# A three-layer interaction network on one core: one more group split by VectorE, a high-part ring of four, loop bodies of four steps

## What is computed

```python
for i, S in enumerate([128, 128, 128]):
    Wr = Ws[i].reshape(39, h.shape[1], S)
    out = relu(einsum('bfd,bgd,fgs->bsd', x, h, Wr) + bs[i][None, :, None])
    if i != 2:
        h, direct = out[:, :64], out[:, 64:]
    else:
        direct = out
    outs.append(direct)
return sum(concatenate(outs, axis=1), axis=-1)
```

## Time and profile before

| | |
|---|---|
| median of 3 runs | 571.18 us (571.01 to 573.93) |
| the profiled execution | 570.96 us, its span 569.1 us |
| busy, share of the span | PE 98%, DVE 93%, POOL 89%, PE's weight loads 66%, ACT 64% |
| granted PE clock | 0.996 of full speed |
| transfers | 121.68 MB, mean 214 GB/s |
| chain that ended last | PE 88%, POOL 5%, issue 3%, DMA, DVE and ACT 1% each |

### The profile page before, as it was taken

How to read it: one execution, slowest core, us unless ns; L and a number is a source line. 1 busy time by engine, 2 the same in 40 slices (tenths; PEclk the granted TensorE clock), 3 DMA queues, 4 the chain that set the end, 5 groups by cost and what they waited for, 6 DMA issues and landing times.

```text
span 569.1 us, 7814 instructions
## 1 busy us (share of the span) xinstructions
PE 558.0 (98%) x2003; PEld 377.6 (66%) x2003; DVE 531.8 (93%) x516; ACT 365.8 (64%) x409; POOL 505.5 (89%) x222
## 2 busy tenths in 40 slices
PE   8899999999999999999999999999999999999997
PEld 4354666767676666667767667676767766666765
DVE  5679999999999999999999999999999999999975
ACT  1255775766767576676776758586676757668562
POOL 1257999899999999999899999989999999999995
PEclk9899999999999999999999999999999999999999
DMA  8998935738375582846649285573837558262001
GB/s 331 412 413 329 383 115 181 299 124 332 101 261 225 179 332 85 311 157 203 276 146 346 68 295 214 166 313 113 329 111 256 229 173 337 79 210 80 0 2 37
DMA packets 27390, 121.68 MB, mean 214 GB/s; under 512 B 3312, under 2 KB 3440, under 8 KB 25328
## 3 DMA queue, kind: packets, MB, share of 16 engines
q1 hardware_dynamic: 27376, 121.52, 58.8%
HBM read 120.98 MB, written 0.52 MB: 213 GB/s over the span
## 4 chain that ended last, share of the span: by engine, by line
PE 88%; POOL 5%; issue 3%; DMA 1%; DVE 1%; ACT 1%; SPq 0%; POOLq 0%; DVEq 0%; ACTq 0%
PE acc L572 88%; POOL z_lo L294 4%; DMA xfirst<-x 1%; POOL w_lo L540 1%; DVE z_whole L431 0%; DVE z_raw L431 0%; ACT h L660 0%; ACT last L660 0%; ACT z_hi L657 0%; SPq L304 0%; SPq L327 0%; DVE z_hi L292 0%; ACT direct L660 0%; DVE sums L454 0%; DVE z_lo L291 0%
## 5 line engine op out<-in xcount | busy, mean ns | idle before, releaser
L294 POOL TENSOR_TENSOR z_lo<-z_raw,z_hi 128x1024 fp32r<-128x1024 f32 x202 | 477.8, 2406 | 25.2 <-ACT z_hi L657 22.7
L657 ACT CAST z_hi<-z_raw 128x1024 fp32r<-128x1024 f32 (+1 forms) x215 | 216.9, 1022 | 111.5 <-DVE z_raw L431 94.0
L431 DVE TENSOR_TENSOR z_raw<-h,xwide 128x1024 f32<-128x1024 f32 x189 | 225.6, 1214 | 4.7 <-ACT h L660 3.0
L572 PE MATMUL acc<-z_hi,w_hi 128*128 128x512 f32 (+1 forms) x543 | 210.1, 460 | 0.8 <-ACT last L660 0.8
L572 PE MATMUL acc<-z_hi,w_lo 128*128 128x512 f32 x530 | 171.7, 395 | 0.0
L572 PE MATMUL acc<-z_lo,w_hi 128*128 128x512 f32 x498 | 160.0, 397 | 2.3 <-POOL z_lo L294 1.9
L572 PEld LDWEIGHTS acc<-z_hi,w_hi 128*128 128x128 f32 (+1 forms) x543 | 102.2, 188 | 60.6 <-issue 39.5
L572 PE MATMUL acc<-z_whole,w_whole 128*128 128x512 f32 x256 | 120.0, 592 | 0.0
L572 PEld LDWEIGHTS acc<-z_hi,w_lo 128*128 128x128 f32 x530 | 99.4, 188 | 24.0
L572 PEld LDWEIGHTS acc<-z_lo,w_hi 128*128 128x128 f32 x498 | 92.6, 187 | 28.4 <-POOL z_lo L294 5.8
L431 DVE TENSOR_TENSOR z_whole<-h,xwide 128x1024 f32<-128x1024 f32 x68 | 82.3, 1213 | 6.2 <-PE acc L572 3.9
(11 more groups left out here) (25 smaller groups left out, 155.1 us busy)
## 6 DMA issues: line engine op xcount, KB each, us to landing
xwide<-x SPq DMA_DIRECT2D x160, 512.0 KB, 4.7
xfirst<-x SPq DMA_DIRECT2D x13, 2048.0 KB, 7.8
xfirst<-x SPq DMA_DIRECT2D x4, 768.0 KB, 12.2
xwide<-w SPq DMA_DIRECT2D x2, 1024.0 KB, 16.7
xwide<-x SPq DMA_DIRECT2D x1, 1280.0 KB, 11.8
xfirst<-x SPq DMA_DIRECT2D x2, 512.0 KB, 11.4
xwide<-x SPq DMA_DIRECT2D x1, 768.0 KB, 9.2
z_raw<-w0b SPq DMA_DIRECT2D x1, 640.0 KB, 6.0
```

The source lines that it names most:

```text
L294: return eng.tensor_tensor(lo[0:rows, 0:n, :], z[0:rows, 0:n, :], hi[0:rows, 0:n, :].bitcast(F32), ALU.subtract)
L431: nc.vector.tensor_tensor(dst, in0, in1, ALU.mult).then_inc(made[kind], 1)
L572: return nc.tensor.matmul(dst, w[0:rows, place, :], z[0:rows, t - G * g, :], start=first and first_g and t == G * g, stop=final and t == T ...
L657: nc.scalar.copy(z_hi[0:rows, slot("PV", pair, par, pos, HI_RING), 0:n, :], src).then_inc(hi_made, 1)
```

## The change

Layer 1's group 3 (position 3) becomes V instead of W. `z_hi` has four slots instead of six. The loop's body holds four steps and turns three times (a step has 19 P and V groups now, and a ring must fit into the loop body a whole number of times). In the first steps:

- Step 0 takes group 4 of layer 1 whole, with the raw weights, ahead of group 5; one P group less.
- Block 1's layer 0 is accumulated in `acc[2]`, so PE does not wait there for ACT to have read `acc[0]`; `relu0` reads it from there, and layer 2's first group in step 1 waits for that read.
- At the end of step 0 ACT runs `copy_xrep(1)` ahead of `relu0`.
- The split of layer 2's weights moves from position 2 of step 1 to position 0 on ACT and POOL, and on ACT ahead of `relu1`; their load moves ahead of one load of layer 0's operands in SP's queue.
- Layer 1 has 18 split weight tiles instead of 16 (and `w_whole` two less), so the staging areas in `xwide` shift and three `xwide` loads of block 1 wait for layer 2's split instead of two.

```diff
-KINDS = ("WPWP", "PWPWPPVPPV", "PPWPVPPWPV")
+KINDS = ("WPWP", "PWPVPPVPPV", "PPWPVPPWPV")
-ORDER_0 = "00W 01W 02W 03W 11W 13W 10W 12W 16W 14P 17W 15P 18P 19V"
-ORDER_1 = ("00W 01W 22W 27W 02W 03W 20P 10P 11W 21P 12P 23P 13W 14P 24V 15P 16V 25P 17P 18P 19V "
+ORDER_0 = "00W 01W 02W 03W 11W 13W 10W 12W 16W 14W 15P 17W 18P 19V"
+ORDER_1 = ("00W 01W 22W 27W 02W 03W 20P 10P 11W 21P 12P 23P 13V 14P 24V 15P 16V 25P 17P 18P 19V "
-SPLIT2_AT_1 = 2
-WHOLE_RING, RAW_RING, HI_RING, LO_RING = 4, 4, 6, 4
+SPLIT2_AT_1 = 0
+WHOLE_RING, RAW_RING, HI_RING, LO_RING = 4, 4, 4, 4
...
             load_first(2, xfirst_head_in[0], range(0, 1 + G))
+            sp.dma_start(stage[2][:, 0:SPLIT_COUNT[2], :], w2).then_inc(w_staged[2], 16)
             load_first(2, xfirst_head_in[1], range(1 + G, 1 + 2 * G))
-            sp.dma_start(stage[2][:, 0:SPLIT_COUNT[2], :], w2).then_inc(w_staged[2], 16)
...
-            with act.Fori(1, PAIRS - 1) as pair:
-                for par in range(2):
-                    step(pair, par)
+            with act.Fori(0, (BLOCKS - 4) // LOOP) as turn:
+                for par in range(LOOP):
+                    step(LOOP // 2 * turn + 1, par)
...
-                dst = acc[layer][:, :]
+                dst = acc[2 if isinstance(j, int) and (layer, j) == (0, 0) else layer][:, :]
...
-                    ready(pe, acc_read[layer], j + (1, 0, -1)[layer])
+                    if isinstance(j, int) and (layer, j) == (2, 1):
+                        pe.wait_ge(acc_read[0], 2)
+                    if isinstance(j, int) and layer == 0 and j < 2:
+                        ready(pe, acc_read[0], j)
+                    else:
+                        ready(pe, acc_read[layer], j + (1, 0, -1)[layer])
...
+                    if isinstance(j, int) and j == 1 and pos == SPLIT2_AT_1:
+                        split_layer(2)
                     if pos == RELU1_AT and has(1, BLOCKS):
-                        relu1(j, par)
+                        relu1(j, par % 2)
...
                 if isinstance(j, int) and j == 0:
-                    relu0(j, par)
                     copy_xrep(1)
+                    relu0(j, par % 2)
```

More of the change, by code:

```diff
@@ L20 @@
 PAIRS = BLOCKS // 2
+LOOP = 4
+assert LOOP % 2 == 0 and (BLOCKS - 4) % LOOP == 0
 BB = N // DIM
@@ L176 @@
 assert sorted(e[:2] for e in BEGIN[0]) == sorted(e[:2] for e in STEP if e[0] < 2)
-assert len(SPLIT0) > 0 and SPLIT_COUNT[1] <= 16 and SPLIT_COUNT[2] <= 16
+assert len(SPLIT0) > 0 and SPLIT_COUNT[1] <= 20 and SPLIT_COUNT[2] <= 16
 def cin(nc, x, x0, w0a, w0b, w1, w2, w_rest, b, out):
@@ L213, in cin @@
         z_psum = psum("z_psum", [128, G, N])
-        stage = [None, xwide[:, 1, T12 - 4:T12, :].rearrange("p a (b s) -> p (a b) s", s=SIZE),
-                 xwide[:, 1, T12 - 8:T12 - 4, :].rearrange("p a (b s) -> p (a b) s", s=SIZE)]
+        stage = [None, xwide[:, 1, T12 - 5:T12, :].rearrange("p a (b s) -> p (a b) s", s=SIZE),
+                 xwide[:, 1, T12 - 9:T12 - 5, :].rearrange("p a (b s) -> p (a b) s", s=SIZE)]
         xsecond = xwide[:, 1, 0:1 + T0, :]
@@ L263, in cin @@
         for kinds, ring in (("W", WHOLE_RING), ("P", RAW_RING), ("PV", HI_RING), ("PV", LO_RING)):
-            assert 2 * sum(e[2] in kinds for e in STEP) % ring == 0
+            assert LOOP * sum(e[2] in kinds for e in STEP) % ring == 0
         def place_of(j, layer):
@@ L339, in _ @@
             load_first(2, xfirst_head_in[0], range(0, 1 + G))
+            sp.dma_start(stage[2][:, 0:SPLIT_COUNT[2], :], w2).then_inc(w_staged[2], 16)
             load_first(2, xfirst_head_in[1], range(1 + G, 1 + 2 * G))
-            sp.dma_start(stage[2][:, 0:SPLIT_COUNT[2], :], w2).then_inc(w_staged[2], 16)
             load_first(2, xfirst_in, range(1 + 2 * G, 1 + T0))
             sp.wait_ge(*made_all(0, 0))
-            for g in range(G12 - 4):
+            for g in range(G12 - 5):
                 load_wide(1, 1, g)
@@ L352, in _ @@
             sp.wait_ge(w2_lo_made, 1)
-            for g in range(G12 - 4, G12 - 2):
+            for g in range(G12 - 5, G12 - 2):
                 load_wide(1, 1, g)
@@ L409, in products @@
                         dve.wait_ge(h_ready[0], 2 * (j + 1))
-                    dve.wait_ge(xw_in[1 - par][g], 16 * (pair + par + 1))
+                    dve.wait_ge(xw_in[1 - par % 2][g], 16 * (pair + par // 2 + par % 2 + 1))
                     in0 = h[0][:, None, :].to_broadcast([128, n, N])
-                    in1 = xwide[:, 1 - par, G * g:G * g + n, :]
+                    in1 = xwide[:, 1 - par % 2, G * g:G * g + n, :]
                 else:
@@ L416, in products @@
                     in0 = h[1][:, None, :].to_broadcast([128, n, N])
-                    in1 = xwide[:, par, G * g:G * g + n, :]
+                    in1 = xwide[:, par % 2, G * g:G * g + n, :]
                 number = before(kind, j, pos)
@@ L462, in step @@
                 if (not isinstance(j, int) or j > 1) and order(j - 1)[-1][2] == "V":
-                    late.append((V_LAG - 1, pair + par - 1, 1 - par, len(order(j - 1)) - 1))
+                    late.append((V_LAG - 1, *((pair, par - 1) if par else (pair - LOOP // 2, LOOP - 1)), len(order(j - 1)) - 1))
                 for pos, (layer, g, kind) in enumerate(order(j)):
@@ L467, in step @@
                     if pos == SUM1_AT and not (isinstance(j, int) and j < 1):
-                        sum_direct(j - 1, par)
+                        sum_direct(j - 1, par % 2)
                     if pos == SUM2_AT and not (isinstance(j, int) and j < 2):
@@ L502, in _ @@
                 step(0, par)
-            with dve.Fori(1, PAIRS - 1) as pair:
-                for par in range(2):
-                    step(pair, par)
+            with dve.Fori(0, (BLOCKS - 4) // LOOP) as turn:
+                for par in range(LOOP):
+                    step(LOOP // 2 * turn + 1, par)
             for par in range(2):
@@ L549, in _ @@
                 step(0, par)
-            with pool.Fori(1, PAIRS - 1) as pair:
-                for par in range(2):
-                    step(pair, par)
+            with pool.Fori(0, (BLOCKS - 4) // LOOP) as turn:
+                for par in range(LOOP):
+                    step(LOOP // 2 * turn + 1, par)
             for par in range(2):
@@ L635, in _ @@
                 step(0, par)
-            with pe.Fori(1, PAIRS - 1) as pair:
-                for par in range(2):
-                    step(pair, par)
+            with pe.Fori(0, (BLOCKS - 4) // LOOP) as turn:
+                for par in range(LOOP):
+                    step(LOOP // 2 * turn + 1, par)
             for par in range(2):
@@ L684, in relu0 @@
                     act.wait_ge(*made_all(j, 1))
-                a = acc[0]
+                a = acc[2 if isinstance(j, int) and j == 0 else 0]
                 relu(h[0][0:HALF, :], a[0:HALF, :], 0, slice(0, HALF)).then_inc(h_ready[0], 1)
@@ L715, in step @@
                     if pos == RELU0_AT and has(1, BLOCKS - 2):
-                        relu0(j, par)
+                        relu0(j, par % 2)
+                    if isinstance(j, int) and j == 1 and pos == SPLIT2_AT_1:
+                        split_layer(2)
                     if pos == RELU1_AT and has(1, BLOCKS):
-                        relu1(j, par)
+                        relu1(j, par % 2)
                     if pos == RELU2_AT and has(2, BLOCKS):
                         relu2(j)
-                    if isinstance(j, int) and j == 1 and pos == SPLIT2_AT_1:
-                        split_layer(2)
                     if kind != "W":
```

## The result

The changed kernel takes 580.69 us (median of 4 runs, 580.43 to 581.26) against 571.10 us; the ratio is 1.016, 95% interval 1.014 to 1.019. The forecast was 581.0 us and slower.

The account below looks back on a forecast made before the run. The loop through POOL, PE and ACT, at 34.80 us a step, was taken to bound the changed kernel: 570.96 + 12.6 for 13 steps - 2.6 for the first steps = 581.0 us, range 573.0 to 585.0.

Parts of the forecast that it names:

- PE 33.53: PE's work per step: position 3 as V instead of W saves 0.31 us, from 33.84 to 33.53.
- DVE 34.20: DVE's work per step: 33.07 us before plus one whole subtraction of 1.13 for position 3.
- the loop 34.80: Closed chain per step from POOL's position 0 through PE, ACT and back to POOL: 33.73 us plus 1.07.
- the added rounding: With four `z_hi` slots, ACT's rounding 20 waits for PE's position 16, ahead of `relu0`: 1.07 us more per step.
- 13 steps: POOL's position 0 in steps 2 to 15, 13 intervals of 34.80: 452.4 against 439.8 us, +12.6.
- first steps: Start: PE's removed wait and slow clock, earlier weight split, against later loads; bounds -1.4 to +4.6, gain of 2.6 us taken.
- from step 15's position 0 to the end of the span: The end: twelve POOL subtractions without a pause set PE's pace and layer 2 is unchanged; 0 us.
- That DVE sets the step: Rival: rounding 20 does not lengthen the loop, leaving DVE's 34.20 us a step; 573.2 us, chance 12%.
- That PE's saving counts: Rival: DVE fits the added 1.13 us into idle time, so PE's 33.53 a step holds; 563.9 us, chance 4%.
- That DVE stalls at the new subtraction: Rival: at position 3 DVE waits for rounding 3 behind `relu2`, making its step 35.27 us; 587.1 us, chance 8%.

Follow-up runs that it names:

- the six-slot kernel: The changed kernel with `z_hi` back at six slots and a loop body of all twelve steps; 572.67 us.
- the kernel with short sums and both moves: Changed kernel, six slots, 15 of 16 terms of each sum left out, `relu0`'s `direct` instruction and `relu2` moved later on ACT; 564.69 us.
- the changed kernel with `direct` moved: Changed kernel, four slots, `relu0`'s third instruction (writes `direct`) moved behind the rounding of the next step's position 0; 573.42 us.
- run 69: Not a label but a count: the kernel before, unchanged, was run 69 times beside the other kernels; from 569.2 to 574.2 us.

## Why the prediction was right

**The cause.** The step was forecast as the longest of three claims, PE 33.53, DVE 34.20 and the loop 34.80, and the loop won. Its links, forecast and measured: POOL's position 0 to PE's end of position 6, 12.44 and 12.47; PE's release of ACT, taken as PE's end plus 0.20, unchanged; the added rounding 1.07 and 0.96; `relu0` to POOL 7.32 and 7.31. Together 34.80 and 34.72. Removing the ring's share (six slots) and shortening the loop elsewhere (`direct`) each brought the time down to 573; adding the ring alone to the old kernel brought it up to 583.

**The sum.**

| term | forecast | measured |
|---|---|---|
| 13 steps | +12.6 | +11.5 (451.3 less 439.8) |
| first steps | -2.6 | -2.6 (76.24 against 78.88) |
| from step 15's position 0 to the end of the span | 0 | +0.5 (50.93 against 50.42) |
| outside the span | 0 | +0.9 (2.76 against 1.86) |

The measured terms are those of the two profiled executions, 581.26 less 570.96, and add up to +10.3 against +10.0.
The rounding was oversized by 0.1 a step: the first `relu0` instruction starts 0.96 after it, where I had used its duration and a gap. The end was costed at nothing, as POOL sets PE's pace there; it lost half a microsecond. There `relu1` started 26.10 us after POOL's position 0 (25.68 before), behind the rounding of position 23, which was late by 1.0. The old kernel with four slots lost 0.3 there (581.0 - 530.30 is 50.70). The 0.9 outside the span belongs to the profiled execution: the four runs of the changed kernel have spans of 578.5 or 578.6, and 1.92, 1.93, 2.36 and 2.76 us outside them. Why it varies is not explained; the other kernels have 1.7 to 2.3. That 581.0 met the median of 580.69 so closely is luck in part, since a step that was too long by 0.08 stands against an end and a remainder that were costed at nothing.

**The first steps.** The value was right and its split was loose: bounded from -1.4 to +4.6 with 2.6 chosen, and that it was met to 0.1 is luck. The forecast read 3.9 us at half the clock with 1.9 lost; finer stretches give 3.4 us and 1.7. `relu1` did wait for the weights' rounding (39.63, right behind 37.70 plus 1.91), and the removed wait gave more than that cost.

**The rivals.** That DVE sets the step is false for this kernel and true as soon as the loop is out of the way; its price, 573.2, is what three kernels measured (572.7 to 573.7). That price was met by luck: their steps are 34.01 to 34.07 and not 34.20, and their ends are longer (570.3 less 518.48 is 51.8 in the six-slot kernel, against 50.4). My 33.07 for DVE was 0.17 too high, since it left a third wait of 0.14 in DVE's work, below. That PE's saving counts needed DVE's room, as the forecast said, and something it didn't say: the second loop too. That DVE stalls at the new subtraction is where I was incomplete. I had seen that rounding 3 stands behind `relu2`, and priced only DVE's wait for it. I missed that rounding 4, and so POOL's position 4, stand behind it as well. In the changed kernel this costs nothing, since the first loop is longer; it would have spoilt a forecast for six slots and less work on DVE.

**The most-contended engine.** The page that says to work on it first (the Trainium skill, Perfetto Trace Analysis, section Identifying the Most-Contended Engine) would have chosen PE here by its matmul busy time, 100% of a middle stretch; it warns of that figure for TensorE and names the busy share of the weight loads as one of two better ones, and with their 69.7% DVE comes first at 97.8%. PE's own work did fall as computed, since 33.53 is the step of the kernel with short sums and both moves, and the changed kernel got slower all the same. The rule names the engine to work on; it gives no price for a change that relieves this engine and lengthens a loop through others.

## What to carry to other kernels

When three engines are over 90% busy, compare not only their work but the closed chains through them: follow one instruction through each wait until it meets its successor a step later, and add up. A slot that comes free is an edge of such a chain; making a ring smaller moves a wait, and the price is what stands behind the waiting instruction on its in-order engine. Such a chain can be shortened for nothing by moving an instruction that nobody is waiting for behind one that somebody is.

## What the runs showed of the hardware

**A wait that no bracket shows.** In the kernel before, 0.73 us pass on DVE from the start of the sum of `direct` to the next product; in the changed kernel and in the one with six slots it is 0.59, for the same instruction of 0.67 to 0.68 us. The product reads `xrep_psum`, which ACT copies. ACT and DVE of the kernel before, then DVE of the kernel before with four slots:

```profile
218.13 0.59 ACT L678 COPY xrep_psum<-xfirst 128x512 f32<-128x512 f32 x1
```

```profile
218.21 0.67 DVE L447 TENSOR_REDUCE sums<-direct 128x512 f32 x1
218.94 1.22 DVE L431 TENSOR_TENSOR z_whole<-xrep_psum,xfirst 128x1024 f32<-128x1024 f32 x1
```

```profile
256.94 0.68 DVE L447 TENSOR_REDUCE sums<-direct 128x512 f32 x1
257.53 1.21 DVE L431 TENSOR_TENSOR z_whole<-xrep_psum,xfirst 128x1024 f32<-128x1024 f32 x1
```

The copy ends at 218.72 and the product starts 0.22 later; in the other five steps from 100 to 300 us it is 0.21 or 0.22 too. With four slots the copy is over at 256.53, before the sum starts, and the distance is 0.59, although DVE waits longer there at position 19. So the 0.14 is a wait for ACT. DVE's need before was 33.84 - 0.77 - 0.14 = 32.93, and with the added subtraction 34.06, where 34.03 was measured.

**The clock.** In the kernel before, PE had waited 0.36 and 0.24 us ahead of its matmuls at 10.33 and 12.53, then stood for 2.19. The granted clock was 0.50 (1.2 GHz) from about 18.35 to 21.76 us, 3.4 us, and full again at 22. In the kernel with only the weight split moved the wait was again 2.19 and the clock fell again; with the wait removed it stayed at 1.00 through the first steps. A shorter wait can stand before a fall too: in the trace of the changed kernel with `direct` moved, PE waited 1.25 and 0.78 us before matmuls at 551.15 and 552.89, and the clock was 0.50 from 553.0 to about 556.4. But five of the ten runs of that kernel have a mean clock of 1.00, and a wait of 1.31 us before the matmul at 10.30 in the changed kernel brought no fall.

The price of a fall can be read from the repeated runs. The kernel before was run 69 times beside the kernels above. Eleven runs with a mean granted clock of 0.999 or 1.000 took 569.2 to 569.5 us, 39 with 0.996 or 0.997 took 570.6 to 571.3, 14 with 0.993 or 0.994 took 572.0 to 572.5, and five with 0.990 or 0.991 took 574.0 to 574.2. The four traces that have the wait of 2.19 us have 0.996 or 0.997, and each shows one fall between 17 and 22 us and the full clock from 24 to 560; where the further falls of the other runs lie was not traced. One fall thus costs about 1.6 us. `acc[2]` alone has a mean clock of 1.00 in all six runs and takes 568.49: of its 2.5 us, 1.6 are the clock's and 0.8 the wait's, if the full-clock runs of the kernel before had that wait as well, which no trace shows. At full clock on both sides the changed kernel is behind by 11.4 us (580.69 against 569.33), not 9.6.
